# Rest probabilities as one stacked operand, and page results gathered page by page

## The chip, the cores and the metric

One core of one Trainium2 chip. The metric is the device time of one execution in microseconds, the median of several runs. The core has five engines that matter here, each with its own queue of instructions in order: TensorE (PE in the rows; PEld is its loading of weights), VectorE (DVE), ScalarE (ACT), GpSimd (POOL), and SyncE (SP), which issues most of the DMAs. They meet through semaphores.

## The reference

A gated cross-attention block and a mixture-of-experts block over 32 batches of 256 tokens with 256 features, all in float32:

```python
x = x + tanh(g_xattn) * xattn(layernorm(x), ctx)      # 16 heads of 64, 77 context rows and one null key/value
x = x + tanh(g_ffn) * ffn(layernorm(x))

# xattn: q = xn @ Wq * 64**-0.5; k, v = split(ctx @ Wkv), each with the null row in addition (78 rows in all)
#        out = softmax(q @ k.T) @ v, heads joined, @ Wout, then a layer norm with ln_scale and ln_bias
# ffn:   32 routed experts, each token's 8 best by sigmoid(x @ Wr + br), weights normalised to sum 1
#        expert(x) = (silu(x @ Wg + bg) * (x @ Wu + bu)) @ Wd + bd, hidden size 128
#        result = shared expert(x) + sum over the 8 of weight * expert(x)
```

## The kernel before

It has three phases. The context phase makes the keys and values of all batches and leaves them in DRAM. The attention phase goes over the batches in a software pipeline. The expert phase then goes over 175 rounds of 512 tokens.

**Products.** Nearly every float32 product is made of three: both operands are split into a high part, which ScalarE makes by a rounding copy, and a low part, which VectorE makes as the difference. `split_product` issues high x high, low x high and high x low.

**Attention.** A step `b` works on batch `b` and, behind it, on the output projection, the layer norms and the routing of the batches before. The order on TensorE is the list `RING`; the results go into four PSUM banks by the table `BANK`, and `free` makes a new entry wait for what its bank held. `EVICTED` is the same list for ScalarE (`high`) and VectorE (`low`). Two entries concern the change. Of the 78 probabilities of a head 64 are "main" and 14 are "rest". T0a to T3a transpose the main ones; T1b and T3b transpose the rest of all 8 heads of a half at once, 112 rows (8 x 14), and both are split into high and low. PV0a to PV1b then multiply with the values: for each of the 8 pairs of heads three main products and three rest products, the rest ones over all 112 rows with values that are zero except in the pair's 28 rows (`v_rest`). T1b and PV0a have bank 1 in common. PV0a's main products wait for T1a, its rest products for T1b.

SyncE issues in a step, in this order: the next `x_in` (which waits for `xn`), a page fill of zeros, the loads of the next batch's `v_main` (2) and `v_rest` (8 small ones, one for a head), a fill, the next batch's keys `kT` (2), the stores of x2T and of the routing weights, `x_res`, a fill, the store of x1 (which waits for `x`, L1063), a fill. In step -1 it also puts the null value's row into both `v_rest` buffers, 16 loads more. In the first three steps a fill is 1.5 MB, later 1 MB and 0.5 MB.

VectorE's order around the change: T1b's low part, `normalise` of units 2 and 3, `centre` (`z`, L1055, which frees bank 3), PV0a's and PV0b's low parts, `placed`, T2a's low part, `residual` (`x`, L1063), T3a's, T3b's. `centre` waits for `rstd`, which POOL makes (`make_rstd`, L831) between its scatters: POOL writes each token's row into its experts' pages with 16 indirect DMAs a batch (L842), and these fill most of its time.

**Experts.** Of the 16 blocks of 512 tokens for the shared expert ("dense" rounds), 12 run first (`EARLY`), then 159 pages, each of 512 rows of one expert, then the 4 blocks of `LATE`. A round's up and gate products run in its own step, its down products one step later, its eviction and the store two steps later. When all pages of a batch have been stored, POOL gathers the eight results of its 256 tokens from DRAM with 16 indirect DMAs (L1702, `parts`, 8 for each tile of 128 tokens), and VectorE adds them with their weights to the dense result in 16 additions (`add_weighted`, L1811), four in a round. The batches of blocks 12 to 14 are summed before their dense round; block 15, the last two batches, is first among the late rounds, and its dense result is stored, loaded again and summed at the very end (`left`).

Of the kernel before, what the change touches and what calls it, by code (L numbers as in the profile page):

```python
# [23 lines left out]
P = 128  # L24
# [76 lines left out]
REST = J - DH  # L101
BUFFERS = 3
# [401 lines left out]
def attention_phase(nc, ctx, across, dram, stores, ident, wq, wo, opened_by, rows, kept, ahead, norm):  # L504
# [81 lines left out]
    probs = [sb(f"probs{i}", [P, PAIRS * J]) for i in range(2)]  # L586
    pT = [sb(f"pT_{s}", [P, HP + 1, N], F32R) for s in "hl"]
# [7 lines left out]
    gate_ready, rows_ready = sem("gate_ready"), sem("rows_ready")  # L595
    x_loaded, res_loaded = sem("x_loaded"), sem("res_loaded")
# [32 lines left out]
    def rest_values(batch, part, half, pair):  # L629
        return v_rest[batch % 2][0:PAIRS * REST, part, half, pair, :]  # L630

# [16 lines left out]
    def destination(name, b):  # L648
# [5 lines left out]
        if name in ("T1b", "T3b"):  # L654
            return ps[0:PAIRS * REST, 0:N], [t[0:PAIRS * REST, HP, :] for t in pT]
# [9 lines left out]
    def sync(sp, dense):  # L665
# [5 lines left out]
        def load_values(batch):  # L671
# [60 lines left out]
        def step(b, par, h):  # L732
# [19 lines left out]
            if b == -1:  # L752
                sp.wait_ge(null_lo, 1)

                for v in v_rest:
                    rest = v[:, :, :, :, :].rearrange("p s f q d -> p (s f) q d")
                    for head in range(PAIRS):
                        sp.dma_start(rest[(head + 1) * REST - 1:(head + 1) * REST, :, head // 2, head % 2 * DH:(head % 2 + 1) * DH].bitcast(F32),
                                     null_rows[:, :, :, :].rearrange("p s f d -> p (s f) d").bitcast(F32)).then_inc(null_placed, 16)
# [36 lines left out]
    def gpsimd(pool, dense):  # L796
# [9 lines left out]
        def prepare():  # L806
# [3 lines left out]
            last.then_inc(zeroed, 1)  # L810
            pool.memset(blank[:, :, :], 0.0).then_inc(blank_made, 1)
# [94 lines left out]
    def scalar(act, dense):  # L906
# [19 lines left out]
        def high(name, b):  # L926
# [83 lines left out]
    def vector(dve, dense):  # L1010
# [14 lines left out]
        def normalise(u, b):  # L1025
# [4 lines left out]
            if n >= 2:  # L1030
                before_b, before_u = divmod(n - 2, UNITS)
                dve.wait_ge(ring_full, nth(RING, "T1b" if before_u < 2 else "T3b", before_b))
            e, inv = exps[u % 2], row_inv[u][:, :].unsqueeze(2)
            main = probs[u % 2][:, 0:PAIRS * DH].rearrange("p (h j) -> p h j", j=DH)
            rest = probs[u % 2][:, PAIRS * DH:PAIRS * J].rearrange("p (h j) -> p h j", j=REST)
            dve.tensor_tensor(main, e[:, :, 0:DH], inv.broadcast_to([P, PAIRS, DH]), ALU.mult)
            dve.tensor_tensor(rest, e[:, :, DH:J], inv.broadcast_to([P, PAIRS, REST]), ALU.mult).then_inc(probs_ready, 1)
# [1027 lines left out]
```

## Time and profile before

| | us |
|---|---|
| median of 3 runs | 2132.0 (2131.1 to 2134.18) |
| the profiled execution | 2131.79 |
| its span | 2130.0 |
| busy in the span: PE / DVE / ACT / POOL | 2009.3 / 1697.5 / 1359.0 / 1205.8 |
| context phase | 0 to about 242 |
| attention phase | about 242 to 1140 |
| expert phase | about 1140 to 2130 |

The phases overlap a little: the first dense rounds run while the last batches' attention ends. A span is counted from the first to the last instruction. Busy times of TensorE are made with modelled ends of the matmuls, which overlap, so a busy share near 100% doesn't say by itself that nothing waits; the chain of waits does. An "issue" in the chain is a time in which an engine waited for nothing that the profile shows. SPq is SyncE's queue of DMA issues: the time of a row is how long the issuing took, not the transfer.

### The profile page before, as it was taken

What the parts mean: (1) busy time and instruction counts of PE and PEld (TensorE: products, weight loads), DVE (VectorE), ACT (ScalarE), POOL (GpSimd) and SP (SyncE); (2) the same over time, 40 slices, a digit from 0 to 9 for tenths busy, and PEclk for the clock granted to TensorE, in tenths of its full rate; (3) what the DMA queues carried; (4) which work ended last, traced back from release to release, by engine and by line L of the source; (5) the groups of instructions that cost most, each with busy time, mean ns of one, the idle gap of its engine ahead of it and who ended that gap; (6) DMA issues with size and microseconds to landing.
All of it is one profiled execution on the core that took longest, in us unless ns stands there. A gap on an engine that the chain in (4) does not pass through costs nothing.

```text
span 2130.0 us, 42507 instructions
## 1 busy us (share of the span) xinstructions
PE 2009.3 (94%) x13730; PEld 1836.1 (86%) x13730; DVE 1697.5 (80%) x4060; ACT 1359.0 (64%) x3966; POOL 1205.8 (57%) x1322
## 2 busy tenths in 40 slices
PE   7999688999999999999996899999999999999994
PEld 7888578999999999999996788888888888888884
DVE  5544257888888888888887766668999999999996
ACT  2211356777777777777773257777777777777771
POOL 0001203777777777777777500007777777777775
PEclk9999899999999999999998899999999999999997
DMA  8664388987777777777787999999999999999997
GB/s 274 214 194 165 124 258 295 305 256 240 244 242 236 241 247 241 240 242 247 239 275 235 314 333 285 287 285 386 402 403 401 397 392 389 402 393 393 396 360 276
DMA packets 400531, 625.60 MB, mean 294 GB/s; under 512 B 170935, under 2 KB 275096, under 8 KB 397848
## 3 DMA queue, kind: packets, MB, share of 16 engines
q1 hardware_dynamic: 351160, 488.60, 67.7%
q0 software_dynamic: 49152, 134.28, 17.5%
q8 instruction: 112, 1.84, 0.4%
q14 instruction: 107, 0.88, 0.1%
HBM read 315.08 MB, written 307.63 MB: 292 GB/s over the span
## 4 chain that ended last, share of the span: by engine, by line
PE 30%; DVE 22%; DMA 14%; POOL 11%; issue 8%; ACT 3%; SPq 1%; DVEq 0%; POOLq 0%; ACTq 0%
DMA w_raw<-in_experts 12%; POOL pages_dram L842 6%; DVE parts L1811 4%; PE ring L140 4%; PE ring L142 3%; PE ring L141 3%; PE xps L1910 2%; DVE minus_max L1022 2%; PE sim L1284 2%; POOL of_key L849 2%; DVE hid_l L1868 2%; DVE w_l L1785 2%; DVE outT_l L1169 2%; POOL x L871 2%; PE yps L140 2%
## 5 line engine op out<-in xcount | busy, mean ns | idle before, releaser
L1702 POOL DMA_INDIRECT parts<-results_dram,kept_index x512 | 518.7, 1013 | 381.3 <-DMA results_dram<-y 220.2
L842 POOL DMA_INDIRECT pages_dram<-rows,kept_index x512 | 509.5, 995 | 167.6 <-issue 139.2
L921 ACT ACTIVATE exps<-sim,minus_max 128x78 f32<-128x78 f32 x1024 | 320.9, 366 | 38.6 <-DVE minus_max L1022 38.6
L921 ACT ACTIVATION_READ_ACCUMULATOR exps<-sim,minus_max 128x1 f32 x1024 | 252.3, 247 | 0.0
L1723 ACT ACTIVATE w_h<-w_raw 128x768 fp32r<-128x768 f32 x159 | 134.0, 843 | 146.8 <-DMA w_raw<-in_experts 146.8
L1811 DVE SCALAR_TENSOR_TENSOR parts<-parts,kept_weight 128x256 f32<-128x256 f32 x448 | 213.5, 476 | 3.2 <-DMA parts<-dense_dram 2.0
L140 PE MATMUL yps<-w_h,hid_h 128*128 128x256 f32 x636 | 181.9, 286 | 4.1 <-DVE hid_l L1868 3.2
L1785 DVE TENSOR_TENSOR w_l<-w_raw,w_h 128x768 fp32r<-128x768 f32 x159 | 151.9, 956 | 38.1 <-ACT w_h L1723 37.9
L1910 PE MATMUL xps<-ident,xin 128*128 128x128 f32 x1272 | 173.4, 276 | 7.9 <-issue 4.9
L142 PE MATMUL yps<-w_l,hid_h 128*128 128x256 f32 x636 | 178.3, 280 | 0.0
L141 PE MATMUL yps<-w_h,hid_l 128*128 128x256 f32 x636 | 177.8, 280 | 0.0
L1730 ACT ACTIVATE y<-yps 128x512 f32<-128x512 f32 x318 | 171.7, 597 | 2.4 <-PE yps L142 2.4
L1284 PE MATMUL sim<-kT,qT 128*128 128x156 f32 x1024 | 154.4, 302 | 11.6 <-issue 7.5
L1754 ACT ACTIVATE hid_h<-up_ps 128x512 fp32r<-128x512 f32 x175 | 103.3, 590 | 89.1 <-DVE up_ps L1862 88.3
L140 PE MATMUL ring<-xnT_h,wq_h 128*128 128x256 f32 x512 | 156.5, 306 | 2.7 <-DVE xnT_l L1169 1.4
L1773 DVE TENSOR_TENSOR wq_l<-xps,wq_h 128x512 fp32r<-128x512 f32 x212 | 142.9, 686 | 18.5 <-ACT wq_h L1717 18.5
L1910 PEld LDWEIGHTS xps<-ident,xin 128*128 128x128 f32 x1272 | 141.4, 141 | 18.4 <-DMA xin<-pages_dram 5.3
L1284 PEld LDWEIGHTS sim<-kT,qT 128*128 128x128 f32 x1024 | 142.3, 193 | 16.5 <-issue 13.8
L140 PE MATMUL ring<-wo_h,outT_h 128*128 128x256 f32 x512 | 148.4, 290 | 3.4 <-DVE outT_l L1169 0.5
L1862 DVE SCALAR_TENSOR_TENSOR up_ps<-up_ps,w_raw,act_gate 128x512 f32<-128x512 f32 x159 | 120.0, 755 | 38.6 <-PE up_ps L142 37.0
L1022 DVE TENSOR_REDUCE minus_max<-sim 128x8 f32<-128x624 f32 x128 | 102.2, 799 | 56.4 <-PE sim L1284 56.3
L141 PE MATMUL ring<-xnT_h,wq_l 128*128 128x256 f32 x512 | 144.3, 282 | 0.0
(258 smaller groups left out, 6643.1 us busy)
## 6 DMA issues: line engine op xcount, KB each, us to landing
xin<-pages_dram SPq DMA_DIRECT2D x159, 512.0 KB, 10.8
results_dram<-y SPq DMA_DIRECT2D x159, 512.0 KB, 9.6
w_raw<-in_experts SPq DMA_DIRECT2D x159, 385.0 KB, 9.3
pages_dram<-blank SPq DMA_DIRECT2D x108, 512.0 KB
pages_dram<-blank SPq DMA_DIRECT2D x12, 1536.0 KB
values_dram<-values SPq DMA_DIRECT2D x16, 1024.0 KB
v_main<-values_dram SPq DMA_DIRECT2D x64, 256.0 KB
keys_dram<-keys SPq DMA_DIRECT2D x16, 616.0 KB, 4.2
```

Of the source, the lines that this page charges most:

```text
L140: eng.matmul(out, left[0], right[0], start=start, stop=False)
L141: eng.matmul(out, left[1], right[0], start=False, stop=False)
L142: return eng.matmul(out, left[0], right[1], start=False, stop=stop)
L842: pool.indirect_dma_start(dram["pages"], bass.IndirectOffsetOnAxis(ap=kept_index[:, at:at + 1].bitcast(U32), axis=0), buffer(batch)[:, k / ...
L921: last = act.activation(exps[u % 2][:, h, :], scores(u)[:, h // 4, h % 4, :], ACT.Exp, bias=minus_max[u][:, h:h + 1], accum_out=row_sum[u] ...
L1022: dve.tensor_reduce(minus_max[u][:, :].rearrange("p (a h) -> p a h", a=2), scores(u), AX.X, ALU.max, negate=True).then_inc(max_done, 1)
L1284: last = pe.matmul(sim[u % 2][:, i // 2, (i % 2) * 2 * J:(i % 2 + 1) * 2 * J], qT[:, pair, tt * P:(tt + 1) * P], kT[:, pair, :], start=Tru ...
L1702: pool.indirect_dma_start(parts[slot(batch, t)][:, k, :], None, done, bass.IndirectOffsetOnAxis(ap=kept_index[:, at:at + 1].bitcast(U32), ...
L1730: last = act.activation(y[s][:, q:q + 2, :], yps[:, q:q + 2, :], ACT.Copy)
L1785: dve.tensor_tensor(w_split[s][1][:, :], w_raw[s][:, 0:EW], w_split[s][0][:, :].bitcast(F32), ALU.subtract).then_inc(w_lo, 1)
L1811: dve.scalar_tensor_tensor(out=out, in0=part[:, k, :], scalar=kept.weight[:, at:at + 1], in1=part[:, TOPK, :], op0=ALU.mult, op1=ALU.add). ...
L1910: last = pe.transpose(xps[:, c, q * P:(q + 1) * P], xin[s][:, q, c * P:(c + 1) * P], ident[:, :])
```

## The change

Rest probabilities: VectorE now writes the 14 rest probabilities of the heads into four strips of 32 columns, one strip for a pair of heads, with zeros in the four columns left over (`probs` ends in 128 columns instead of 112). The transposes T1b and T3b give 128 rows. A new operand `pR` holds, for two pairs each, the high part in the 64 rows in which it came and the low part in the other 64 rows. `v_rest` holds the values of a pair in both halves of the rows. One product with the high values then gives high x high and low x high together, so that a pair takes two products instead of three; the second, with the low values, also adds low x low. ScalarE and VectorE evict T1b and T3b in two pieces of 64 rows each. Each batch's `v_rest` takes 16 loads instead of 8, the null rows 32 instead of 16.

`centre` waits for the mean and variance only; the wait for `rstd` moves to `residual`.

Gathers: the chosen results of a token are held in the order of their pages, the last page first. So choice k can be gathered k pages before the batch's last page is stored. POOL now goes page by page, and after each page gathers what can be had: choices k and k + 4 of two neighbouring batches, 4 gathers (2 at the first and the last four pages). They go to 5 buffers `got`, and VectorE adds them a fixed number of rounds later (`BEHIND`: page p in round p + 17, six rounds after the page's own) to `totals` of 3 batches. Loads of dense results and stores of sums are 256 KB instead of 128 KB. Block 15 moves to the early rounds, block 11 becomes late; the batches of blocks 11 to 14 are all summed before their dense round, and the loads of the late rounds go before the store in SyncE's step.

The diff, cut to its core:

```diff
-LATE = (15, 12, 13, 14)
+LATE = (11, 12, 13, 14)
 EARLY = DENSE - len(LATE)
-SUMMED_FIRST = range(BATCHES * min(LATE), BATCHES * max(LATE))
+BLOCKS = [n for n in range(DENSE) if n not in LATE] + list(LATE)
+SUMMED_FIRST = range(BATCHES * min(LATE), BATCHES * (max(LATE) + 1))
+GOT, TOTALS = 5, 3
+BEHIND = EARLY + 5
...
-    probs = [sb(f"probs{i}", [P, PAIRS * J]) for i in range(2)]
-    pT = [sb(f"pT_{s}", [P, HP + 1, N], F32R) for s in "hl"]
+    probs = [sb(f"probs{i}", [P, PAIRS * DH + P]) for i in range(2)]
+    pT = [sb(f"pT_{s}", [P, HP, N], F32R) for s in "hl"]
+    pR = sb("pR", [P, 2, N], F32R)
...
+    def rest_rows(head):
+        first = head // 2 % 2 * STRIP + head % 2 * REST
+        return [slice(first + side, first + side + REST) for side in (0, HALF)]
...
             for head in range(PAIRS):
                 col = head % 2 * DH
-                sp.dma_start(rest[head * REST:(head + 1) * REST - 1, :, head // 2, col:col + DH].bitcast(F32),
-                             by_head[DH:M, :, head, :]).then_inc(values_loaded[batch % 2], 16)
+                for strip in rest_rows(head):
+                    sp.dma_start(rest[strip.start:strip.stop - 1, :, head // 2, col:col + DH].bitcast(F32),
+                                 by_head[DH:M, :, head, :]).then_inc(values_loaded[batch % 2], 16)
...
                     for head in range(PAIRS):
-                        sp.dma_start(rest[(head + 1) * REST - 1:(head + 1) * REST, ...
+                        for strip in rest_rows(head):
+                            sp.dma_start(rest[strip.stop - 1:strip.stop, ...
...
+            if name in ("T1b", "T3b"):                       # ScalarE
+                for side in range(2):
+                    strip = slice(side * HALF, (side + 1) * HALF)
+                    last = act.activation(pR[strip, side, :], bank(name, b)[strip, 0:N], ACT.Copy)
+                return signal(last)
...
         def centre(b):
-            dve.wait_ge(rstd_done[1], b)
+            dve.wait_ge(aggregated[1], b)
...
         def residual(b, par):
             dve.wait_ge(biased, b)
             dve.wait_ge(applied[1], b)
+            dve.wait_ge(rstd_done[1], b)
...
+            if name in ("T1b", "T3b"):                       # VectorE
+                for side in range(2):
+                    strip, other = slice(side * HALF, (side + 1) * HALF), slice((1 - side) * HALF, (2 - side) * HALF)
+                    last = dve.tensor_tensor(pR[other, side, :], bank(name, b)[strip, 0:N], pR[strip, side, :].bitcast(F32), ALU.subtract)
+                return signal(last)
...
                 for i, pair in enumerate(pairs):
-                    last = split_product(pe, ps[:, i * N:(i + 1) * N], [rest_values(b, part, half, pair) for part in range(2)],
-                                         [t[0:PAIRS * REST, HP, :] for t in pT], start=False, stop=i == 1)
+                    for part in range(2):
+                        last = pe.matmul(ps[:, i * N:(i + 1) * N], rest_values(b, part, half, pair), pR[:, pair // 2, :],
+                                         start=False, stop=i == 1 and part == 1)
...
+    def choices(pages):
+        spread_over = N * TOPK // PAGE
+        of = [(k, divmod(pages + k - opened_pages(0), spread_over)) for k in range(TOPK)]
+        return [(batch, k) for k, (batch, part) in of if part == 0 and 0 <= batch < B]
+    first_gather = opened_pages(0) - (TOPK - 1)
...
+        for pages in range(first_gather, OPENED + 1):        # POOL
+            last_round, slot = EARLY + pages - 1, got_slot(pages)
+            for n in range(last_round - (DEPTH - 1 if pages == first_gather else 0), last_round + 1):
+                pool.wait_ge(stored[n % DEPTH], 16 * (n // DEPTH + 1))
+            if pages - GOT >= first_gather:
+                pool.wait_ge(added, additions(pages - GOT + 1))
+            for j, (batch, k) in enumerate(choices(pages)):
+                for t in range(TT):
...
+        def add_weighted(n, i):                              # VectorE
+            pages = n - BEHIND
...
+            if i == 0:
...
+                dve.wait_ge(got_loaded[slot], got_by(pages))
...
+            if EARLY + OPENED <= n + 2 < ROUNDS:             # SyncE
+                load_x2(*moved_by(turn, s, 2))
+                load_x1(*moved_by(turn, s, 2))
             if exists(turn, s, -2):
                 store(*moved_by(turn, s, -2))
```

## Rows read from the trace of the kernel before

**Rows 1.** Busy time by stage: us, each engine's busy (instructions), PE clock, DMA share, GB/s

```profile
437.00:1106.00 669.00, 662.84 (x5351) 640.61 (x5351) 591.36 (x1843) 504.35 (x2112) 514.79 (x598) 1.00 0.78 243
1433.60:2075.00 641.40, 634.11 (x3896) 548.20 (x3895) 600.55 (x1074) 472.84 (x849) 488.19 (x480) 1.00 1.02 392
```

**Rows 2.** SyncE's queue, start of attention: start us, us, engine line op out<-in, count

```profile
251.51 7.15 SPq L683 DMA_DIRECT2D v_rest<-values_dram  x8
258.70 9.85 SPq L758 DMA_DIRECT2D v_rest<-null_rows  x16
...
272.87 8.78 SPq L683 DMA_DIRECT2D v_rest<-values_dram  x8
...
282.25 2.02 SPq L669 DMA_DIRECT2D kT<-keys_dram  x2
...
365.41 2.01 SPq L669 DMA_DIRECT2D kT<-keys_dram  x2
```

**Rows 3.** Chain of waits, first products of batches 1 and 4: start us, us, what

```profile
283.47 6.58 issue
290.05 2.43 PE sim L1284 x8
...
379.83 1.08 PE sim L1284 x8
```

**Rows 4.** Waits of SyncE's queue, 600 to 1000 us: us in total, times, longest

```profile
SPq L781 <- DVE x L1063: 105.5, 15, 7.5
SPq L744 <- ACT xn L955: 36.1, 15, 2.5
```

**Rows 5.** Chain of waits through one batch in the attention loop: start us, us, what

```profile
837.33 1.08 PE sim L1284 x8
...
855.10 0.73 POOL rstd L831
...
857.38 0.66 PE ring L1335 x4
...
858.37 0.12 PE ring L141
...
864.16 1.08 PE sim L1284 x8
```

**Rows 6.** ScalarE's and VectorE's timelines in that batch (T1b's eviction, `centre`)

```profile
852.18 0.41 ACT L933 ACTIVATE pT_h<-ring 112x256 fp32r<-112x256 f32 x1
...
852.69 0.43 DVE L1169 TENSOR_TENSOR pT_l<-ring,pT_h 112x256 fp32r<-112x256 f32 x1
853.03 0.19 DVE L1028 RECIPROCAL row_inv<-row_sum 128x8 f32<-128x8 f32 x1
...
855.86 0.88 DVE L1055 SCALAR_TENSOR_TENSOR z<-ring,mean_var,scale_row 128x256 f32<-128x256 f32 x2 [0.69 <-POOL rstd L831]
```

**Rows 7.** Chain of waits, the end: start us, us, what

```profile
2070.05 0.63 PE xps L1903 x4
...
2073.21 0.25 PE up_ps L142
...
2073.70 12.28 DMA wq_l<-x2T_l_dram
...
2086.53 0.23 PE gate_ps L141
...
2091.23 1.29 DVE y L1794 x2
```

**Rows 8.** Stores' landing (KB, median us; the first from 1600 to 2000); one gather, its addition

```profile
results_dram<-y SPq DMA_DIRECT2D x75, 512.0 KB, 9.7
...
out_dram<-y SPq DMA_DIRECT2D x3, 512.0 KB, 4.3
...
1615.78 0.94 POOL L1702 DMA_INDIRECT parts<-results_dram,kept_index  x1 [0.30 <-issue]
...
1624.08 0.47 DVE L1811 SCALAR_TENSOR_TENSOR parts<-parts,kept_weight 128x256 f32<-128x256 f32 x1
```

More of the change, by code:

```diff
@@ L629, in rest_values @@
     def rest_values(batch, part, half, pair):
-        return v_rest[batch % 2][0:PAIRS * REST, part, half, pair, :]
+        return v_rest[batch % 2][:, part, half, pair, :]
+    def rest_rows(head):
+        first = head // 2 % 2 * STRIP + head % 2 * REST
+        return [slice(first + side, first + side + REST) for side in (0, HALF)]
     def buffer(batch):
@@ L810, in prepare @@
             last.then_inc(zeroed, 1)
+            for p in probs:
+                last = pool.memset(p[:, PAIRS * DH:], 0.0)
+            last.then_inc(pads_zeroed, 1)
             pool.memset(blank[:, :, :], 0.0).then_inc(blank_made, 1)
@@ L1590, in load_x1 @@
                     source = dense_tiles
-                    for t in range(TT):
-                        sp.wait_ge(out_stored[t], 16 * (batch + 1))
+                    sp.wait_ge(out_stored, 16 * (batch + 1))
                 else:
@@ L1671, in sync @@
         yield from rounds(step)
-        for batch in left:
-            for t in range(TT):
-                load_dense(batch, t)
-        store_out(left[0] - 1, 1)
-        load_x1((ROUNDS - 1) // DEPTH, (ROUNDS - 1) % DEPTH)
-        for t in range(TT):
-            store_out(left[0], t)
-            store((ROUNDS - 2 + t) // DEPTH, (ROUNDS - 2 + t) % DEPTH)
-        for t in range(TT):
-            store_out(B - 1, t)
-        for t in range(TT):
-            sp.wait_ge(out_stored[t], 16 * B)
+        for n in range(ROUNDS - 2, ROUNDS):
+            store(n // DEPTH, n % DEPTH)
+        store_out(B - 1)
+        sp.wait_ge(out_stored, 16 * B)
         for s in range(DEPTH):
@@ L1731, in evict, with step @@
             last.then_inc(act_out, 1)
[L1733 removed]
+        def step(turn, s):
             n = number(turn, s)
@@ L1795, in evict @@
             last.then_inc(dve_out, 1)
-        def add_weighted(batch, t, k):
-            part, before = parts[slot(batch, t)], (TOPK - 1) * (batch * TT + t)
-            at = (batch * TT + t) * TOPK + k
-            if k == 0:
-                if batch == 0 and t == 0:
+        def add_weighted(n, i):
+            pages = n - BEHIND
+            if not first_gather <= pages <= OPENED or i >= TT * len(choices(pages)):
+                return
+            (batch, k), t, slot = choices(pages)[i // TT], i % TT, got_slot(pages)
+            at, total = (batch * TT + t) * TOPK + k, totals[batch % TOTALS][:, t, :]
+            if i == 0:
+                if pages == first_gather:
@@ L1803, in add_weighted @@
                     dve.wait_ge(kept.summed, B)
-                dve.wait_ge(dense_loaded[slot(batch, t)], 16 * (batch // 2 + 1))
-                dve.wait_ge(parts_loaded[slot(batch, t)], 16 * TOPK * (batch // 2 + 1))
-            else:
-                dve.wait_ge(added, before + k)
-            if k == TOPK - 1 and batch:
-                dve.wait_ge(out_stored[t], 16 * batch)
-            out, done = (part[:, TOPK, :], added) if k < TOPK - 1 else (out_rows[t][:, :], combined[t])
-            dve.scalar_tensor_tensor(out=out, in0=part[:, k, :], scalar=kept.weight[:, at:at + 1], in1=part[:, TOPK, :],
-                                     op0=ALU.mult, op1=ALU.add).then_inc(done, 1)
@@ L1829, in find_owners @@
+            if k == 0 and batch:
+                dve.wait_ge(out_stored, 16 * batch)
+            dve.scalar_tensor_tensor(out=total if k else out_rows[:, t, :], in0=got[slot][:, i // TT, t, :],
+                                     scalar=kept.weight[:, at:at + 1], in1=total, op0=ALU.mult, op1=ALU.add).then_inc(added, 1)
         def find_owners(i):
@@ L1882, in vector @@
         yield from rounds(step)
-        for t in range(TT):
-            sum_tile(left[0], t)
-            step((ROUNDS + t) // DEPTH, (ROUNDS + t) % DEPTH)
-        for t in range(TT):
-            sum_tile(B - 1, t)
+        for n in range(ROUNDS, ROUNDS + 2):
+            step(n // DEPTH, n % DEPTH)
+        for n in range(ROUNDS + 2, OPENED + BEHIND + 1):
+            for i in range(TT):
+                add_weighted(n, i)
     def tensor(pe):
```

161 lines of the change are left out of this document (65 added, 96 removed).

## Prediction, made before the result was known

> **What bounds the kernel now.** I read the busy time by stage first [rows 1]. From 437 to 1106 us (the attention loop) TensorE is busy 662.84 of 669 us, from 1434 to 2075 (pages and gathers) 634.11 of 641.4, there with the DMA engines at a share of 1.02. That looks like a TensorE bound, but ends of matmuls are modelled, so I went on to the chain of waits inside one batch. Its steps [rows 5] run sim, POOL's `rstd`, VectorE's `z` [rows 6], and only then TensorE: a loop of 864.16 - 837.33 = 26.83 us in which VectorE idles 0.69 us for `rstd` [rows 6] and TensorE waits for VectorE to free a bank. So a batch is bound by a POOL-VectorE-TensorE loop, with TensorE close behind. The third view is the start of attention, on SyncE's own queue [rows 2] and in the chain [rows 3]: TensorE sits 6.58 us until 290.05 without a named releaser, and the one operand of these products that had been issued late is the keys `kT` of batch 1, issued from 282.25 to 284.27. Landing therefore took at most 5.8 us. Here SyncE's issuing sets the pace, not TensorE. The last view is the end [rows 7]: the last page's products stop at 2073.46 and the span ends at 2130.0; the first thing between them is a 12.28 us load, for which TensorE stands still.
>
> **Part 1, products.** One product in three of the rest goes: 8 of 24 a batch. Back to back a product of 256 columns takes 0.12 us of TensorE's time [rows 5] (not the 0.28 of its own span), so 0.96 us a batch if TensorE sets the pace. On the way in, each of T1b and T3b is evicted as two halves of 64 rows instead of one piece of 112. Such an instruction's time goes with its 256 columns as far as the nearest rows tell, so I take no rebate for fewer rows; below nothing it can't fall, since no instruction leaves. ScalarE's one took 0.41, VectorE's 0.43 with the next starting 0.34 later [rows 6]. VectorE's half starts when both ScalarE halves are done: ScalarE ends 0.32 later (estimate: 0.41 less the same overlap), so VectorE starts at 853.01 instead of 852.69, and takes 0.34 more: 0.66 us late. TensorE's PV0a shares T1b's bank and waits as well: the four products saved in PV0a and PV0b pay for that wait.
>
> **Part 2, `centre` no longer waits for `rstd`.** VectorE's idle 0.69 goes and `z` could start at 855.17; with the 0.66 above it starts at 855.83, hardly earlier than 855.86 now. The wait moves to `residual`, after T2a's eviction; `rstd` ends at 855.83 [rows 5], over 2 us before that, so it costs nothing; if POOL were later, T2a's successors on VectorE (T3a, T3b, statistics) would queue behind it. The old loop is broken, and what is late next is VectorE's own queue. After T3a four products less remain: 0.03 + 4 x 0.12 = 0.5 us a batch. Ends: 0.2 if T3b's halves hold PV1a too, 0.96 if nothing of the evictions is on the path. Over 25 batches: -12.5 us (-5 to -24).
>
> **Part 3, the loads of `v_rest`, doubled.** The high and the low rows need the same values twice, so each batch has 16 loads instead of 8, and the null rows 32 instead of 16. All are issued by SyncE in order, ahead of the keys. Eight took 7.15 us (batch 0) and 8.78 us (batch 1), the 16 null ones 9.85 [rows 2]. Queued behind them: page fills, `kT`, x2T stores, x_res, x1's store, the next x_in. In the middle of the loop this is hidden: in 600 to 1000 us SyncE waited 105.5/15 = 7.0 us for `x` and 36.1/15 = 2.4 us for `xn` a batch [rows 4], 9.4 against some 8 more, so 1.4 are left; if that cover were gone, every batch would pay. At the start it isn't: before the keys of batch 1 stand 7.15 + 9.85 + 8.78 = 25.8 us more, and batch 1 starts at 316 instead of 290. Three more batches add about 8 each before the keys of batch 4, 49.8 in all; of that 379.83 - 365.41 - 2.01 - 5.8 = 6.6 us were slack [rows 2, 3]. That is 43, and two more (estimate) until SyncE, whose waits are now gone, has caught up: +45 us. Ends: 50 if no slack helps; 19 if the three 8s vanish in time in which the queue is full of page fills anyway (25.8 - 6.6).
>
> The rows say that SyncE is held for 0.9 us by each of these 13 KB loads, one behind the other [rows 2]. The Trainium skill (DMA: Bandwidth & Descriptors, section "Issuing engines are not separate DMA queues") calls the time on the sequencer to initiate a DMA "usually small relative to the DMA itself"; by that the 45 would be near 0 and the kernel faster, which is the second rival. I go by the rows.
>
> **Part 4, gathers page by page.** The 512 gathers, their bytes and the 512 additions stay; POOL's first gather comes seven pages earlier, and at the last page two are left instead of 32. In the stage, 480 gathers in 641.4 us [rows 1] are 1.336 us each, 5.34 a page of four. Pages run at the same 5.34, so POOL keeps up and I put the stage at 0. The new wait is VectorE's for a page's gathers six rounds after the page: behind it on VectorE stand the x, w and hidden evictions that all of the expert work needs. Storing starts two rounds after the page, so 4 x 5.34 = 21.4 us are there for the store (9.7), four gathers (5.34) and the last one's landing, which may take 6.3 us. Its landing isn't shown; the tightest of the 64 pairs (a tile's last gather and the first addition of it, none of which waited) is a gather that ended at 1616.72 and its addition at 1624.08 [rows 8]: at most 7.4, and no less than nothing. I take a value under 6.3, in the upper part of that span, and so no wait; the stage's ends are 0 and the +34 of rival (c).
>
> **Part 5, the end.** Block 15 moves to the early ones, so no dense result has to be stored, loaded and summed at the end. From 2073.46: the last page's down products 12 x 0.12 = 1.4, four dense rounds of 12 x 0.23 [rows 7] + 16 x 0.12 + 0.63 of transposes = 5.3 each, 2 us of waiting for the first x2 load (its loads are issued one round earlier than now), eviction 1.29, store 4.3 [rows 7, 8]: 2073.5 + 1.4 + 21.2 + 2 + 1.3 + 4.3 = 2103.7; 2.8 for the hidden layer between the last up and down products (estimate: three VectorE and ScalarE steps of up to 0.9, as in [rows 6]): 2106.5. Page 159's two gathers and additions lie beside that. -23.5 us (-19 if the x2 loads take 12.28 as now, -27 without the waiting).
>
> **Sum.** On the profiled execution: 2130.0 + 45 - 12.5 - 23.5 = 2139 of span, and 1.8 around it as now (2131.79 in all, median of the runs 2132.0): **2141 us**.
>
> **Rivals.** (a) *The page fills hide the later loads* (end 19 of part 3): 2131.8 + 19 - 12.5 - 23.5 = 2115. For it: in those batches the queue is also full with fills. Against: the keys of batch 1 landed within 5.8 us, so the queue was nearly empty when they came. (b) *Issuing is hidden, the change is all gain*: 2131.8 - 12.5 - 23.5 = 2096. Against: TensorE's 6.58 us [rows 3]. It decides if batch 1 starts before 300. (c) *VectorE waits for gathers in each round*: if the last gather lands 7.4 us after its issue, four rounds need 9.7 + 5.34 + 7.4 = 22.4 us, 5.6 a page instead of 5.34; over some 128 pages +34: 2175. It decides from 6.3 us of landing. (d) *The halves don't do what they should*: products fall, but batches keep 26.8 us because evictions eat all: 2153; it lies within the range.
>
> **How the numbers follow.** Forecast 0.50, (a) 0.19, (b) 0.08, (c) 0.17, (d) 0.06. The range reaches over (a) and (d) and leaves out (b) and the worse part of (c): 2108 to 2172. A measurement of this kernel can tell some 0.2% (4.3 us) from no change. With 8 us of uncertainty around 2141, the forecast is slower in 0.34, within 0.2% in 0.11 and faster in 0.05 of all cases; (a) and (b) are faster, 0.27; (c) and (d) slower, 0.23. So faster 0.32, same 0.11, slower 0.57.
>
> **What would show it.** In the changed profile: batch 1's first products near 316 us, `v_rest` issues of some 16 us between v_main and fills, batch 4 near 420; then a period of 26.3 us; `z` without a wait for `rstd`; no VectorE wait for gathers; an end some 33 us behind the last page's products. I am wrong if the first batches start where they do now, if VectorE's additions wait, or if the period stays at 26.8.

## The result, and the profile after

The changed kernel takes 2234.35 us (median of 4 runs, 2230.5 to 2238.59), the kernel before beside it 2132.96: a ratio of 1.048 (95% interval 1.046 to 1.050). The sign of the forecast was right, the size was not: 101 us slower instead of 9, far outside the range. I read where the time went in the order of the phases.

**The start of attention.** SyncE's queue (columns as in [rows 2]), and TensorE's first products of batches 1 and 4, which answer to [rows 3]; in brackets how long the engine had been idle, and for what:

```profile
251.32 13.45 SPq L694 DMA_DIRECT2D v_rest<-values_dram  x16
264.81 19.60 SPq L770 DMA_DIRECT2D v_rest<-null_rows  x32
...
289.54 15.37 SPq L694 DMA_DIRECT2D v_rest<-values_dram  x16
...
305.52 2.02 SPq L679 DMA_DIRECT2D kT<-keys_dram  x2
```

```profile
313.27 3.93 PE L1314 MATMUL sim<-kT,qT 128*128 128x156 f32 x16 [16.17 <-issue]
...
415.22 1.14 PE L1314 MATMUL sim<-kT,qT 128*128 128x156 f32 x4 [2.12 <-issue]
```

Each `v_rest` load still holds SyncE for 0.8 to 1.0 us, and there are twice as many ahead of the keys. Batch 1 starts 23 us later than in [rows 3] (forecast 26), batch 4 35 later.

**The attention loop.** As a landmark I take `centre`'s `z`, once a batch; the sixth and the 31st are 25 batches apart. Then one batch of VectorE around T1b (it answers to [rows 6]):

```profile
500.62 0.88 DVE L1079 SCALAR_TENSOR_TENSOR z<-ring,mean_var,scale_row 128x256 f32<-128x256 f32 x2
...
839.76 0.86 DVE L1196 TENSOR_TENSOR pR<-ring,pR 64x256 fp32r<-64x256 f32 x2 [0.16 <-ACT pR L950]
...
842.52 0.27 DVE L1060 TENSOR_TENSOR probs<-exps,row_inv 128x112 f32<-128x112 f32 x1
842.82 0.88 DVE L1079 SCALAR_TENSOR_TENSOR z<-ring,mean_var,scale_row 128x256 f32<-128x256 f32 x2
...
1217.23 0.88 DVE L1079 SCALAR_TENSOR_TENSOR z<-ring,mean_var,scale_row 128x256 f32<-128x256 f32 x2
```

`z` follows `probs` without a wait for `rstd`, as meant. But a batch takes (1217.23 - 500.62) / 25 = 28.66 us; 26.9 in the kernel before, 26.3 in the forecast. SyncE's queue over one batch, and all that it waited for between 600 and 1000 us (against [rows 4]):

```profile
825.38 0.93 SPq L755 DMA_DIRECT2D x_in<-in_x  x1
826.36 1.15 SPq L707 DMA_DIRECT2D pages_dram<-blank  x1
827.55 2.67 SPq L689 DMA_DIRECT2D v_main<-values_dram  x2
830.27 15.49 SPq L694 DMA_DIRECT2D v_rest<-values_dram  x16
...
846.36 2.07 SPq L679 DMA_DIRECT2D kT<-keys_dram  x2
...
853.75 1.11 SPq L755 DMA_DIRECT2D x_in<-in_x  x1
```

```profile
SPq L689 <- PE ring L1417: 1.1, 1, 1.1
SPq L779 <- DVE pT_l L1199: 1.0, 3, 0.4
SPq L779 <- DVE pR L1196: 0.9, 2, 0.5
```

The 9.4 us of waiting a batch are down to nothing. From one `x_in` to the next the queue issues without a pause for 853.75 - 825.38 = 28.4 us: SyncE is full, and it sets the batch.

**The page stage.** The stage windows answer to [rows 1]: the second one has TensorE at 624.95 of 664 us, and the DMA rate at 376 GB/s instead of 392.

```profile
531.00:1200.00 669.00, 618.90 (x4815) 588.83 (x4815) 595.82 (x1770) 491.21 (x2010) 493.56 (x564) 0.98 0.75 233
1526.00:2190.00 664.00, 624.95 (x3821) 540.87 (x3819) 592.23 (x1072) 462.70 (x834) 517.79 (x474) 1.00 1.01 376
```

VectorE's waits from 1526 to 2190 us (us in total, times, longest):

```profile
DVE totals L1829 <- DMA got<-results_dram,kept_index: 52.5, 47, 3.0
DVE out_rows L1829 <- DMA got<-results_dram,kept_index: 15.5, 19, 2.1
```

And the gathers as a group, 1526 to 2060 us, in the changed kernel and then in the kernel before (count, us in all, mean ns of one, idle time ahead of them):

```profile
L1717 POOL DMA_INDIRECT got<-results_dram,kept_index x384 | 416.5, 1085 | 118.9 <-issue 107.6 <-DVE totals L1829 7.3 <-DMA results_dram<-y 2.8
```

```profile
L1702 POOL DMA_INDIRECT parts<-results_dram,kept_index x400 | 408.6, 1022 | 125.9 <-issue 125.9
```

VectorE does wait for gathers, and POOL issues them one behind the other: 1.085 + 118.9 / 384 = 1.395 us each, 5.58 for the four of a page, where the kernel before has 1.336 and 5.34.

**The end** is shorter, as forecast. From the last page's hidden layer (2074.9 us before, 2204.6 after) to the end of the span it is 32.2 us instead of 55.1.

### The profile page after: what moved, and what is told of

The parts are those of the page before. It is cut to its first block, busy times and chain, and to the rows that moved or that the text cites. A ratio compares the mean times of both kernels' runs of the same rounds, so it can differ in the third digit from the quotient of the medians.

```text
span 2236.8 us, 42358 instructions
## 1 busy us (share of the span) xinstructions
PE 2014.2 (90%) x13474; PEld 1830.1 (82%) x13474; DVE 1749.0 (78%) x4124; ACT 1384.5 (62%) x4030; POOL 1252.9 (56%) x1324
## 4 chain that ended last, share of the span: by engine, by line
PE 31%; DVE 19%; issue 12%; POOL 11%; ACT 8%; DMA 6%; SPq 1%; DVEq 0%; POOLq 0%; ACTq 0%
POOL got L1717 11%; DMA got<-results_dram,kept_index 6%; ACT exps L936 4%; PE ring L145 3%; PE sim L1314 3%; PE ring L147 3%; PE ring L146 3%; DVE minus_max L1042 2%; PE xps L1913 2%; DVE outT_l L1199 2%; DVE totals L1829 2%; DVE probs L1059 2%; PE gate_ps L145 1%; PE ring L1385 1%; PE yps L145 1%
## 5 line engine op out<-in xcount | busy, mean ns | idle before, releaser
L1717 POOL DMA_INDIRECT got<-results_dram,kept_index x512 | 555.5, 1085 | 361.9 <-DMA results_dram<-y 209.8
L857 POOL DMA_INDIRECT pages_dram<-rows,kept_index x512 | 519.6, 1015 | 240.0 <-issue 143.4
L1829 DVE SCALAR_TENSOR_TENSOR totals<-got,kept_weight,totals 128x256 f32<-128x256 f32 x448 | 213.0, 476 | 54.8 <-DMA got<-results_dram,kept_index 54.1
L1913 PE MATMUL xps<-ident,xin 128*128 128x128 f32 x1272 | 180.4, 277 | 43.5 <-DVE wq_l L1788 21.2
L1314 PE MATMUL sim<-kT,qT 128*128 128x156 f32 x1024 | 167.1, 318 | 56.0 <-issue 46.4
L1314 PEld LDWEIGHTS sim<-kT,qT 128*128 128x128 f32 x1024 | 152.8, 205 | 64.6 <-issue 55.4
L953 ACT ACTIVATE outT_h<-ring 128x512 fp32r<-128x512 f32 x128 | 76.1, 594 | 118.2 <-PE ring L1385 105.7
```

The lines of the kernel that those rows point to most:

```text
L857: pool.indirect_dma_start(dram["pages"], bass.IndirectOffsetOnAxis(ap=kept_index[:, at:at + 1].bitcast(U32), axis=0), buffer(batch)[:, k / ...
L1314: last = pe.matmul(sim[u % 2][:, i // 2, (i % 2) * 2 * J:(i % 2 + 1) * 2 * J], qT[:, pair, tt * P:(tt + 1) * P], kT[:, pair, :], start=Tru ...
L1717: pool.indirect_dma_start(got[slot][:, j, t, :], None, dram["results"][0:pages * PAGE, :], bass.IndirectOffsetOnAxis(ap=kept_index[:, at:a ...
L1829: dve.scalar_tensor_tensor(out=total if k else out_rows[:, t, :], in0=got[slot][:, i // TT, t, :], scalar=kept.weight[:, at:at + 1], in1=t ...
L1913: last = pe.transpose(xps[:, c, q * P:(q + 1) * P], xin[s][:, q, c * P:(c + 1) * P], ident[:, :])
```

## Experiments

The table has, for each kernel, the period of a batch (start of the 31st `z` less that of the sixth, by 25) with the sixth `z` for the start, and the time of a round between the `hidden` steps (L1862 before, L1865 after) of the 65th and the 171st round (106 rounds, pages with gathers; the 171st is the last page). The ratio is to the kernel before in the same group of runs, with its 95% interval.

| kernel | sixth z, us | batch, us | round, us | median, us | ratio |
|---|---|---|---|---|---|
| before | 452.2 | 26.90 | 5.30 | 2132.96 | |
| after | 500.6 | 28.66 | 5.65 | 2234.35 | 1.048 (1.046 to 1.050) |
| att_only | 501.0 | 28.56 | 5.33 | 2222.12 | 1.043 (1.041 to 1.045) |
| exp_only | 452.0 | 26.89 | 5.63 | 2141.12 | 1.005 (1.003 to 1.006) |
| more_loads | 498.9 | 28.24 | 5.31 | 2211.23 | 1.038 (1.037 to 1.040) |
| centre_only | 447.6 | 26.60 | 5.31 | 2121.11 | 0.996 (0.994 to 0.997) |
| fewer_loads | 449.4 | 26.79 | 5.62 | 2134.7 | 1.002 (1.001 to 1.003) |
| merged | 458.0 | 26.77 | 5.60 | 2145.62 | 1.008 (1.005 to 1.010) |
| spread | 492.1 | 27.38 | 5.65 | 2188.67 | 1.026 (1.022 to 1.030) |
| whole_evict | 449.2 | 25.66 | 5.67 | 2112.93 | 0.992 (0.990 to 0.994) |
| behind6 | 501.6 | 28.68 | 5.53 | 2225.18 | 1.045 (1.044 to 1.047) |
| merged_behind6 | 461.8 | 26.80 | 5.61 | 2141.1 | 1.005 (1.003 to 1.006) |
| low_psum | 451.7 | 26.87 | 5.34 | 2115.67 | 0.993 (0.991 to 0.995) |
| before_low_psum | 452.3 | 26.88 | 5.34 | 2130.7 | 0.999 (0.998 to 1.000) |
| apart | 451.4 | 26.87 | 5.36 | 2115.77 | 0.993 (0.991 to 0.994) |
| merged_apart | 460.0 | 26.78 | 5.35 | 2119.42 | 0.995 (0.993 to 0.996) |
| best1 | 449.1 | 26.60 | 5.36 | 2105.88 | 0.988 (0.986 to 0.990) |

**Cut in two.** Each half of the change alone, on the other half of the kernel before.

> The attention part of the change alone (stacked rest probabilities, 16 v_rest loads a batch, centre without the wait for rstd), with the expert phase of the kernel before. In the changed kernel the first dense round came 94.8 us later than before. Theory Q (SyncE's queue is full: 26 us later keys for batch 1, some 48 by batch 6, then a period of 28.5 us instead of 26.9): 2132 + 94 = 2226 us, and the queue shows no wait over 1.1 us between 600 and 1000 us. Theory X (the later loss comes from an interplay with the new expert phase, which allocates other buffers): the start's 45 us stay, the period is 26.3 and the time about 2165.

> The expert part alone (gathers page by page, five buffers, blocks 11 to 14 late), with the attention phase of the kernel before. Theory G (VectorE waits for gathers in each round, 5.6 to 5.7 us a page instead of 5.34, and the end is 23 us shorter): 2132 + 36 - 23 = 2145 us. My prediction's reading (the page stage costs nothing, and what was seen comes from the late attention): 2132 - 23 = 2109 us, and no wait of VectorE for got.

Against their kernel before of 2131.59 us they are +90.5 and +9.5, 100 together, where the whole change is 101. The halves don't disturb each other, theory X and the prediction's reading of the page stage fall, and each can be studied alone.

**Only the loads.** The kernel before with every `v_rest` load issued twice:

```diff
+ sp.dma_start(rest[PAIRS * REST:(PAIRS + 1) * REST - 1, :, head // 2, col:col + DH].bitcast(F32), by_head[DH:M, :, head, :])...
```

> The kernel before with nothing but twice the v_rest loads: each of the 8 loads of a batch is issued a second time, into rows 112 to 124 which no product reads, and the 16 null loads a second time into row 125. Products, evictions and centre are those of before. Theory Q (issuing alone makes the loss): the first products of batch 1 near 313 us, a period of 28 to 28.5 us, and 2132 + 94 = 2226 us. Rival E (the evictions in halves make the longer period, SyncE only the late start): period 26.9, 2132 + 48 = 2180 us. My prediction's cover (9.4 us of SyncE's waits hide 8 more): the same 2180.

The start (46.7 us late at the sixth `z`) is that of the changed kernel, and the period rises to 28.24 us with products and evictions as they were. So issuing alone makes 80 of the 91 us; rival E falls as the main cause, and so does my cover. What SyncE still waited for most in 600 to 1000 us is 3.4 us in all:

```profile
SPq L746 <- ACT xn L959: 3.4, 3, 1.9
```

**Only `centre`.**

> The kernel before with only the wait for rstd moved from centre to residual. My prediction's step (VectorE's 0.69 us of idle time goes, and TensorE is next late): up to 0.69 us in each of some 29 batches, 2112 us; with products as they were and TensorE at 662.84 of 669 us at most 0.24 us a batch, 2125 us. Rival (POOL, or VectorE's queue, sets the pace and the idle time only moves): 2132 us, with residual waiting for rstd.

11 us faster: 0.30 us a batch, and 4.6 ahead of the sixth `z`. That is between the two sizes of my step; the rival falls.

**Fewer loads, the same bytes in fewer loads, and another order.** fewer_loads takes only the first strip of each head (`rest_rows(head)[:1]`); merged brings two heads with one load; spread puts the second strips behind `x_res`.

```diff
-            for head in range(PAIRS):
+            for head in range(PAIRS // 2):
...
-                    sp.dma_start(rest[strip.start:strip.stop - 1, :, head // 2, col:col + DH].bitcast(F32),
-                                 by_head[DH:M, :, head, :])...
+                    sp.dma_start(rest[strip.start:strip.stop - 1, :, head // 2::2, col:col + DH].bitcast(F32),
+                                 by_head[DH:M, :, head::PAIRS // 2, :])...
```

> The changed kernel with the values of the rest loaded into the upper 64 rows only where the head's first strip lies: 8 v_rest loads a batch and 16 null ones, as before the change. The second strip of each head stays zero, so the output lacks the products of one part of the rest probabilities; all products, evictions and gathers run as in the changed kernel. Theory Q (SyncE's issuing is the whole loss of the attention loop): the start of before, a period of 26.3 us by my prediction's steps, so 2234 - 94 - 12 = 2128 us. Rival E (the halves of the evictions cost more than the four saved products give, as the 11 us between the attention part alone and the doubled loads alone suggest): the start of before, a period of 26.9 to 27.1, 2140 to 2148 us.

> The changed kernel, complete, but one load brings the rest values of heads h and h + 4, which go to the same rows of different pairs: 8 loads of 26 KB a batch instead of 16 of 13 KB (the 32 null loads stay). Theory D (a load costs SyncE its 0.98 us whatever is in it; v_main's with 256 KB took 0.76): SyncE has 7.8 us a batch less to issue, the period falls to that of the kernel with fewer loads, and only the null loads (some 10 us more than before the change) stay of the late start: 2234 - 94 - 12 + 10 = 2138 us. Rival B (the cost goes with the rows and pieces of a load): 8 loads take 15.6 us as the 16 did, 2234 us.

> The changed kernel with all its loads, but each head's second v_rest load is issued behind x_res instead of directly behind the first, so the 16 stand in two blocks of 8 with the keys and the stores between them. Theory B (the issues of x_in, fills and v_main grew by 3.4 us a batch because they now follow each other without a pause; with 8 small loads between the large transfers they shrink): SyncE needs some 25.5 us a batch, the period falls to 26.8 us and the keys are 8 us earlier: 2234 - 94 - 3 + 15 (null rows and the first batches) = 2152 us. Theory S (SyncE has 28.2 us of issues a batch wherever they stand): the period stays at 28.2, only the start gets better by 10 to 25 us: 2209 to 2224 us.

SyncE's queue in merged: eight loads of 26 KB take what eight of 13 KB take, and the page fill that follows `x_dram` is again followed by a pause (837.34 to 839.89).

```profile
836.87 0.47 SPq L707 DMA_DIRECT2D pages_dram<-blank  x1
839.89 0.37 SPq L755 DMA_DIRECT2D x_in<-in_x  x1
...
842.63 7.80 SPq L694 DMA_DIRECT2D v_rest<-values_dram  x8
...
851.05 1.51 SPq L679 DMA_DIRECT2D kT<-keys_dram  x2
```

The price is one for each load, not for its bytes or pieces: theory D holds and B falls. With 8 loads, of either kind, the period is 26.8 us, and merged's start is 8.5 us behind that of fewer_loads, which has 16 null loads less (19.60 / 32 = 0.61 us each). So the steady loss is SyncE's, and all of it goes with the issues. The period doesn't fall to 26.3, though, so a second step of mine failed too (below). spread lies between its theories: the start stays late (39.8 us at the sixth `z`), but the loop returns to 27.38 in the mean, with 26.8 in most batches. In spread the queue between two `v_main` loads looks like this:

```profile
830.66 2.62 SPq L689 DMA_DIRECT2D v_main<-values_dram  x2
833.33 8.64 SPq L699 DMA_DIRECT2D v_rest<-values_dram  x8
...
847.12 6.64 SPq L699 DMA_DIRECT2D v_rest<-values_dram  x8
...
857.72 2.87 SPq L689 DMA_DIRECT2D v_main<-values_dram  x2
```

So the order matters for the longer issues, though not for all of them: `v_main`'s are still long. SyncE pauses here as little as in the changed kernel (4.4 us of waiting in all between 600 and 1000 us, 3.0 there), yet its issues take 25.7 us a batch instead of 27.2: issuing without a pause isn't by itself what makes them long.

**The saved products without the halves.** As fewer_loads, but T1b and T3b evicted whole:

```diff
-                for side in range(2): ...
+                return signal(act.activation(pR[:, 0, :], bank(name, b)[:, 0:N], ACT.Copy))            # ScalarE
+                return signal(dve.tensor_tensor(pR[:, 1, :], bank(name, b)[:, 0:N], pR[:, 0, :].bitcast(F32), ALU.subtract))   # VectorE
```

> The changed kernel with 8 v_rest loads a batch (the second strips stay zero) and with T1b and T3b evicted by one instruction of 128 rows on ScalarE and one on VectorE, high part and low part in the same rows; the output lacks the products of one part of the rest probabilities. Products as in the changed kernel. Theory H (the halves, 0.35 us on ScalarE and 0.43 us on VectorE an eviction, eat what 8 products of 0.12 us a batch give): the period falls from 26.78 to 25.8 to 26.2 us, 2135 - 15 to 25 = 2110 to 2120 us. Theory N (TensorE is not what a batch waits for once centre is free): 26.6 as with centre alone, 2130 us.

Theory H holds, by a little more than it said. ScalarE's two halves in the changed kernel (VectorE's 0.86 us are shown at 839.76 above), then ScalarE's and VectorE's instruction here, once in an eviction:

```profile
838.97 0.76 ACT L950 ACTIVATE pR<-ring 64x256 fp32r<-64x256 f32 x2
```

```profile
856.28 0.40 ACT L948 ACTIVATE pR<-ring 128x256 fp32r<-128x256 f32 x1
```

```profile
856.78 0.42 DVE L1191 TENSOR_TENSOR pR<-ring,pR 128x256 fp32r<-128x256 f32 x1
```

The period is 25.66 us: 0.94 less than with `centre` alone, which is the 8 products by 0.12 us; the halves cost 26.79 - 25.66 = 1.13 and give it all back.

**One round more for the gathers** (`BEHIND = EARLY + 6`).

> The changed kernel with the additions one round later (page p in round p + 18, seven rounds after the page's own). Theory G (VectorE waits because store, four gathers and landing take some 22.8 us, four rounds of 5.7): five rounds of 5.34 are 26.7, no wait for got is left, 5.34 us a page, 2234 - 36 = 2198 us. Rival P (POOL's gathers or the DMA engines' rate set 5.7 us a page, whenever the additions come): 2234 us, with POOL or the store later instead. If the end pays for one round more, 5 us at most come on top.

> Both edits of the two runs above. If they are independent, as the attention and the expert part alone were (91 + 10 us against 101 together): 2138 - 36 = 2102 us, faster than the kernel before. If the page stage is bound by POOL: 2138.

Theory G, which was my rival (c), falls: 9 us, not 36, and POOL's gathers still follow each other without a pause and take 5.53 us a round. More distance only delays the point at which VectorE has caught up with POOL: its first wait for `got` comes at 1799 us instead of 1625. merged_behind6 gained no more over merged than 4.5 us. So POOL itself had become slower, and the question was why.

**Who lengthens a gather.** In the changed kernel's trace I set each gather beside VectorE's instruction at its start. Here POOL's gathers, then VectorE's instructions of the same stretch:

```profile
1909.01 0.95 POOL L1717 DMA_INDIRECT got<-results_dram,kept_index  x1 [0.30 <-issue]
1910.26 2.10 POOL L1717 DMA_INDIRECT got<-results_dram,kept_index  x1 [0.30 <-issue]
1912.66 0.95 POOL L1717 DMA_INDIRECT got<-results_dram,kept_index  x1 [0.30 <-issue]
```

```profile
1910.19 0.47 DVE L1829 SCALAR_TENSOR_TENSOR totals<-got,kept_weight,totals 128x256 f32<-128x256 f32 x1
1910.59 0.95 DVE L1800 TENSOR_TENSOR w_l<-w_raw,w_h 128x768 fp32r<-128x768 f32 x1
1911.46 0.68 DVE L1871 TENSOR_TENSOR hid_l<-up_ps,hid_h 128x512 fp32r<-128x512 f32 x1
1914.17 0.48 DVE L1829 SCALAR_TENSOR_TENSOR totals<-got,kept_weight,totals 128x256 f32<-128x256 f32 x1 [2.03 <-DMA got<-results_dram,kept_index]
```

The gather at 1910.26 starts inside an addition that is followed directly by `w_l`; both read two operands from SBUF. It ends at 1912.36, 0.82 us after the end of `w_l` (1911.54), as if it had begun anew there. Then VectorE's next additions wait 2.03 us for it. From 1600 to 2060 us, 167 gathers met such a stretch 0.13 us after their start: mean 1.252 us, up to 2.11, and 113 of them end 0.77 to 0.87 us after the stretch does; the other 159, beside instructions that read one operand from PSUM or beside none: 0.947. `w_l` itself stays at 0.95 us in the mean. Three kernels test it: low_psum gives `w_l`'s place to an instruction with one operand in PSUM (its products lack the low part of the weights), before_low_psum does the same to the kernel before, and apart only moves an addition.

```diff
-            add_weighted(n, 3)                          # apart: between hidden and w_low
...
             dve.tensor_tensor(hid[s % 2][1][:, :], ...  # hid_l
+            add_weighted(n, 3)
```

> The expert part alone, as before, but the low part of the weights is not their difference: VectorE writes, in two instructions of 384 columns, a comparison of a PSUM tile with the high weights in its place, so that this step takes about its old 0.95 us but reads one operand from SBUF instead of two. The output is not the reference's. Theory L (a gather that starts while VectorE runs an instruction with both operands in SBUF waits for its end; in the expert part alone each gather that started inside w_l took 0.82 us plus what was left of w_l, the others 0.95; POOL runs without a pause, so its 4 x 1.40 us a page are the page's time): gathers of 0.95 to 1.0 us, 5.1 to 5.2 us a page instead of 5.63, 2141 - 45 to 55 = about 2090 us. Theory G (store, four gathers and landing set the page's time): gathers a little shorter, at most 10 us gained, 2131. Rival V (VectorE's own 5.0 us a round set it): no gain, 2141 to 2150 us.

> The expert part alone with the round's fourth addition moved from in front of w_l to behind hid_l: the two no longer stand back to back, all work stays. Theory L: the longest stretch of VectorE with both operands in SBUF falls from 1.35 to 0.87 us, no gather is longer than 0.82 + 0.95 = 1.8 us (2.1 now), and the mean falls from 1.09 to some 1.05: 0.16 us a page over 125 pages, 2121 us. Theory G: the same 2141 us.

> The kernel before with the same edit as the first run of this group (the low part of the weights replaced by a comparison with one operand in PSUM; the output is not the reference's). Theory L says that the page stage of the kernel before was POOL's already: its gathers took 1.02 us in the mean and followed each other without a pause, 4 x 1.336 = 5.34 us a page, where the pages ahead of the first gathers took 5.08. Then the stage falls to 5.08 to 5.15: 120 pages by 0.2, 2132 - 24 = 2108 us. If TensorE set the stage in the kernel before, as I took it in the prediction: 2132 us.

The gathers as a group, 1700 to 2000 us: the expert part alone, then low_psum, then apart.

```profile
L1689 POOL DMA_INDIRECT got<-results_dram,kept_index x215 | 235.3, 1094 | 65.5 <-issue 60.3 <-DVE totals L1801 4.3 <-DVE out_rows L1801 0.9
```

```profile
L1689 POOL DMA_INDIRECT got<-results_dram,kept_index x224 | 219.6, 980 | 80.8 <-issue 59.8 <-DMA results_dram<-y 20.0 <-DVE totals L1805 0.9
```

```profile
L1689 POOL DMA_INDIRECT got<-results_dram,kept_index x224 | 218.4, 975 | 82.5 <-issue 58.1 <-DMA results_dram<-y 21.6 <-DVE totals L1801 2.5
```

Both bring the gathers to 0.98 us, POOL waits for stored pages again (20 us), and the median falls by 25 us; the 106 rounds take 568.3 us in apart, where the expert part alone has 597.2 and the kernel before 562.4. Theory L holds for the loss; its bound of 5.1 us a round does not. low_psum, apart and before_low_psum all stop at 5.34 to 5.36, with the kernel before at 5.30: shorter gathers give nothing there. ScalarE's wait in the kernel before, 1700 to 2000 us, and apart's stage window point to what holds them:

```profile
ACT w_h L1723 <- DMA w_raw<-in_experts: 80.5, 56, 2.7
```

```profile
1433.60:2075.00 641.40, 626.70 (x3865) 545.87 (x3864) 598.21 (x1084) 471.39 (x842) 470.01 (x481) 1.00 1.03 393
```

ScalarE waits in each round for a load of weights, and the DMA engines move 393 GB/s, as the 392 of [rows 1]. I read the stage before as the DMA engines', with POOL just behind, though no run moves fewer bytes, so that isn't shown. That the same stage after was POOL's is: shorter gathers alone make it faster.

**Both mends, and a better kernel.** merged_apart is the changed kernel with the merged loads and the moved addition. best1 has the rest probabilities as before, `centre` without `rstd`, the new expert phase with the moved addition, and `BEHIND` one larger.

> The changed kernel, complete, with both mends: 8 loads of 26 KB for the rest values instead of 16, and the fourth addition of a round behind hid_l. If the two causes are what was lost: 2145.6 (loads merged) - 25 (apart) = 2120 us, 0.5% faster than the kernel before. If they overlap, 2130 or more.

> Before's rest probabilities, centre without the wait for rstd, the new expert phase with the fourth addition apart from w_l and the additions one round later. If the parts add: 2132 - 10.5 (centre) + 9.5 (expert part) - 20 (apart, by theory L) - 9 (one round later) = 2102 us. If the page stage is bound as in theory G, one round later is all that helps: 2122.

merged_apart is 2119.42 us, as added up from the two mends (2120): with them the loss is gone and the change is 11 us faster than the kernel before. best1, 2105.88 us, beats both kernels.

## Why the prediction was wrong

**Part 1, products, wrong by the halves.** I put VectorE's T1b chain 0.66 us late and let four saved products "pay for that wait". An eviction in halves costs ScalarE 0.76 instead of 0.41 us and VectorE 0.86 instead of 0.43, so the sizes were near; but it is on a batch's path, twice a batch, and costs 1.13 us in all, where the eight products give 0.94 (whole_evict). In the steady loop the part is worth nothing; I had put half of it on the gain side.

**Part 2, `centre`, right.** `z` waits no longer; alone it gives 0.30 us a batch and 11 us in all. My -12.5 for parts 1 and 2 together came to -5.5 at the 31st `z` where SyncE is out of the way (fewer_loads, 1119.2 against 1124.7 us).

**Part 3, the loads, right at the start and wrong in the loop; this is the step that carries the error.** Batch 1 came at 313.3 (forecast 316), batch 4 at 415.2 (420), and at the sixth `z` the delay was 48 us (45). In the loop I set 8 us of new issues against 9.4 of waits and left 1.4. The 8 were near (8 more loads, 7.3 us). What I left constant was the rest of the queue: without a pause `x_in` takes 0.9 to 1.1 us where it took 0.37 in the kernel before, `v_main`'s two 2.3 to 2.7 instead of some 1.5, the fills 0.9 in the mean instead of 0.6. Added up over the whole batches between 600 and 1000 us, SyncE's issues take 16.1 us a batch before and 27.2 after, and the short gaps between them 0.8 and 1.3. Of the 11.1 more the `v_rest` loads explain 7.3 and the longer issues of the others 3.8; without the 3.8 the queue would have needed 24.7 us. With them the sum, 28.5, goes over 26.9, the period becomes SyncE's own, and "every batch would pay" came true: 25 x 1.76 = 44 us more instead of 12.5 less. That the longer issues come from issuing without a pause isn't shown: in spread the queue pauses as little, and yet the same loads in two blocks brought most batches back to 26.8 us, while `v_main`'s issues stayed long. What exactly they wait for stays open.

The Trainium skill (DMA: Bandwidth & Descriptors, section "Issuing engines are not separate DMA queues") calls this time usually small beside the DMA. The trace agrees where it shows a landing: in the changed kernel's loop a load of keys is issued in 0.83 us and lands after 4.4, a fill in 0.91 and 4.6; for `v_rest` it shows none. But small beside one DMA isn't small in sum: one load of 13 KB and one of 26 KB both hold SyncE for some 0.97 us, and twice the `v_rest` and null loads were 80 of the 101 us lost (more_loads). Going by the rows, and giving rival (b) little, was right.

**Part 4, gathers, wrong, though rival (c)'s price was met.** The stage cost 36 us in the whole change (598.8 instead of 562.4 us for 106 rounds), (c) said 34, and VectorE does wait for gathers. But (c)'s mechanism isn't it: it took gathers of 5.34 us a page and a late landing. In the expert part alone a gather lands after 6.0 us in the median (below (c)'s 6.3) and a store after 6.8 (not 9.7), and one round more changed little. The failed step is "POOL keeps up": I took POOL's 1.336 us a gather as a property of the gather. It was 0.95 of its own, 0.31 between two and 0.07 of waiting for VectorE's two-operand instructions, and the change raised the last to 0.14. POOL needs 5.0 us of a page's 5.34 without it, so it had little room, and as VectorE now waits for POOL in about every second round (66 times from 1526 to 2190 us), a late gather holds the pages up. The Trainium skill (SBUF — State Buffer, section "SBUF: two separate sides") states such a lock between a VectorE instruction with two SBUF inputs and a GpSimd instruction that reads SBUF: whichever comes first holds the port pair for the whole instruction. The gather reads its indices, `kept_index`, from SBUF, and the trace agrees for the gathers (0.947 us against 1.252); that VectorE is held by a gather it doesn't show, `w_l` keeps its 0.95 us. I had read the row's mean without asking what it was made of. The new order doesn't meet many more of the two-operand stretches than the old one (167 of 326 gathers against 163 of 345, 1600 to 2060 us); it meets longer ones. An addition stands directly in front of `w_l` in 78 of 82 rounds, in the kernel before in 38 of 86, and the 33 gathers that start in such an addition take 1.81 us, there 1.04 (also 33). That this pair makes the long gathers is shown by apart. VectorE's waits for the high weights, from 1433 to 2075 us before and from 1526 to 2190 after, tell what stood between the two instructions:

```profile
DVE w_l L1785 <- ACT w_h L1723: 30.3, 52, 1.5
```

```profile
DVE w_l L1800 <- ACT w_h L1738: 1.6, 2, 1.1
```

Whether these waits went because the rounds had become longer, or the other way round, isn't settled.

**Part 5, the end, right.** -23.5 forecast, 32.2 - 55.1 = -22.9 measured. Even the 2 us of waiting are there; TensorE's waits in the late rounds:

```profile
2209.33 0.50 PE L145 MATMUL gate_ps<-wq_h,shared_h 128*128 128x512 f32 x1 [0.16 <-DMA wq_l<-x2T_l_dram]
2216.16 0.50 PE L145 MATMUL gate_ps<-xT_h,shared_h 128*128 128x512 f32 x1 [1.44 <-DMA xT_l<-x2T_l_dram]
2222.16 0.50 PE L145 MATMUL gate_ps<-wq_h,shared_h 128*128 128x512 f32 x1 [1.04 <-DMA wq_l<-x2T_l_dram]
```

**The sum** again, with what was measured: 2130.0 + 48 (start) + 44 (loop) + 36.5 (pages) - 23 (end) = 2235.5; the profiled span is 2236.8. The rivals (a) and (b) are out: nothing was hidden at the start. (d)'s price is out too, as the loop neither gained nor stayed, but its mechanism was right: with 8 loads the batch takes 26.8 us, because the halves eat what the products give (fewer_loads, whole_evict). What the range lacked was the case in which both covers fail at once; I had named the first in a clause, without a price or a chance.

## What to carry to other kernels

Slack in a queue that is nearly full is no cover to the last microsecond: when the pauses went here, the other entries grew too, so add the change to the sum of all issues with their unhurried and their crowded durations, and give the case in which it runs over a price and a chance. Merge small loads first: the issue cost by the load here, whatever was in it. Split the mean of an operation into what it needs and what it waits for before calling it a rate, and where GpSimd issues DMAs, don't put two VectorE instructions that read two SBUF operands each back to back.

## What the runs showed of the hardware

- SyncE's time for a load went by the load: 0.97 us for 13 KB and for 26 KB of 256-byte pieces, 0.75 to 1.3 for 256 KB of `v_main`.
- A gather that GpSimd issued while VectorE read two operands from SBUF ended, in 113 of 167 cases, 0.77 to 0.87 us after that stretch; beside instructions with an operand in PSUM it took its 0.95 us. Moving one addition behind two other instructions was worth 25 us of 2141.
- An instruction on 64 of 128 rows cost about as much as one on all: 0.76 us for two ScalarE halves against 0.40 for one whole, 0.86 against 0.42 on VectorE.
